# Cross-attention on one core: where chunk sums, shares, halves and weighted sums stand, and what they wait for

## The chip, the cores and the metric

The kernel runs on one core of a Trainium2 chip. The metric is device time in microseconds; the time before is the median of three runs. The core's engines are TensorE (PE in the views; its weight loads are PEld), VectorE (DVE), ScalarE (ACT), GpSimd (POOL) and SyncE (SP, here a queue of DMAs). Each works through its own list of instructions in order; semaphores order them among each other.

## The reference

```python
a = layer_norm(ctx, gamma, beta)                    # ctx: 32 x 375 x 512
Q = heads(x @ Wq.T); K = heads(a @ Wk.T); V = heads(a @ Wv.T)     # x: 32 x 112 x 512, 16 heads of 32
scores = einsum('bhtd,bhsd->bhts', Q, K) * 32 ** -0.5
attn = softmax(where(mask, scores, -inf))           # over the 375 context rows
out = heads_joined(einsum('bhts,bhsd->bhtd', attn, V)) @ Wo.T
return x + tanh(gate) * out
```

All is float32. The three projections of the main loop are made of three matmuls each, with high and low parts of both operands (`PASSES`).

## The kernel before

After a start (weights, queries of all sequences, kept in DRAM) comes a loop over 32 sequences of context, c, each with four slots of four heads. Two slots make a pair, m = 2c (even) or 2c + 1 (odd), 64 in all. Every engine has its own `slot_pair(m)`, written out by hand as one order, and they are skewed: what belongs to slots 2m and 2m + 1 on TensorE is exponentiated one pair later and weighted three pairs later.

**TensorE** (line 1291): K projection of slot 2m (12 matmuls into bank KB), V projection of one third of the context, or the output of an earlier sequence (12 into bank VO), K of slot 2m + 1, then a second V third (even m) or the output product `output(c - 3)` (odd m), the weighted sums of slots 2m - 6 and 2m - 5 (48 small matmuls into KB, line 1247) and the scores of 2m and 2m + 1 (line 1234). Outputs are tiles of 128 rows and sequences have 112, so `tile_of(b)` gives no tile for every eighth sequence: in the odd pairs 3, 5, 7 (nothing to put out yet), 23, 39 and 55 there is no output product. K of an even slot waits for the copy of the weighted sums out of KB (`pv_out`), the weighted sums wait for the copy of K out of KB (`k_done`). The last pair has the output of sequence 28 between its two K products.

**ScalarE** (line 804): exponentials of slot 2m - 3, second V copy or gated output, copy of the weighted sums (line 777, `weighted_out`; line 784 at the end), score copies with mask and scale (line 727), K copy (line 741), the high half of the normalised output of sequence c - 3 (line 754, even m), V copy (line 747), high part of the context (line 688), K copy, exponentials of slot 2m - 2 (line 736).

**VectorE** (line 1038): in odd pairs statistics of a later context (line 881) and the shares of sequence c - 2 (lines 986 to 992: adds up the parts, takes reciprocals, transposes), then joined maxima (line 947), row maxima of this pair's scores (line 961), spread (line 952) and subtraction (line 971) of the pair before, partial sums of the chunk sums (line 979).

**GpSimd** (line 594): sums of the three chunks of exponentials of slots 2m - 4 and 2m - 3 (lines 587 and 591, into one of two buffers `psum`), then in even pairs the product with the shares (line 567, `normalised`), the bias on the residual (line 553), the low half (line 575) and row statistics; in odd pairs the result (line 559). Then low parts of the context (line 547).

**SyncE** (line 452): the softmax maxima go through DRAM (`store_maxima`, `load_maxima`, lines 406 and 416), and so do the partial sums of a sequence (`store_parts`, `load_parts`, lines 423 and 430, even m) and the shares (`store_shares`, `load_shares`, lines 436 and 444, odd m). A wait on this queue holds all behind it.

The last three sequences (from `SUMMED` = 29 on) don't go through parts and shares: TensorE makes the denominators from the chunk sums (line 1254), VectorE reduces and spreads their reciprocals into `rspread` (`normalise`, lines 996 to 1002), and GpSimd multiplies (line 570). `o_norm` counts GpSimd's products, `o_done` its low halves.

## Time and profile before

| | us |
|---|---|
| median of 3 runs | 919.99 (919.9 to 923.03) |
| the profiled execution | 922.26 |
| its span, first to last instruction | 920.5 |
| matmuls on TensorE | 899.1 (98%) |
| VectorE / ScalarE / GpSimd | 760.7 / 678.3 / 630.1 |
| granted TensorE clock, mean | 0.996 |

The profile and its trace show one execution. Busy is what an engine executes; an idle time in brackets stands before the instruction that ended it, with the instruction that released it. Matmuls overlap, so their busy time isn't TensorE's peak, and the distance between equal groups is the better clock.

### The profile page before, as it was taken

The numbers are of one execution on the slowest core, as the hardware profiler recorded it, in microseconds if no ns is written. First come the engines' busy times: TensorE is split into PE (matmuls) and PEld (weight loads), VectorE is DVE, ScalarE is ACT, GpSimd is POOL, SyncE is SP. The second block draws the span as 40 slices with busy tenths as digits, with TensorE's granted clock in tenths as the row PEclk, the third lists the DMA queues.
The fourth block names the chain that finished last, engine by engine and source line by source line (L and its number), as shares of the span: only waits on it lengthen the run. The fifth ranks groups of instructions, "written<-read, shape, count | busy, mean of one in ns | idle before, by whom it ended". The sixth has DMA issues, their size and how long they took to land.

```text
span 920.5 us, 25302 instructions
## 1 busy us (share of the span) xinstructions
PE 899.1 (98%) x9747; PEld 780.0 (85%) x9747; DVE 760.7 (83%) x1498; ACT 678.3 (74%) x1304; POOL 630.1 (68%) x730
## 2 busy tenths in 40 slices
PE   8999999999999999999999999999999999999977
PEld 7899888888888888888888888888888888888865
DVE  6963398989888889888888888988888988988757
ACT  3422588878878778888878777877887877877854
POOL 0671466777777777687777677578787776677664
PEclk9999999999999999999999999999999999999989
DMA  9973143434455434445544444445555444544212
GB/s 283 367 245 151 48 98 99 110 95 110 117 128 132 114 104 104 121 117 132 133 114 104 122 125 108 111 102 125 131 133 132 113 102 127 125 101 105 66 31 68
DMA packets 109964, 114.03 MB, mean 124 GB/s; under 512 B 45716, under 2 KB 87604, under 8 KB 109844
## 3 DMA queue, kind: packets, MB, share of 16 engines
q1 hardware_dynamic: 109268, 111.49, 45.2%
q8 instruction: 77, 1.26, 0.6%
q10 hardware_dynamic: 576, 0.92, 0.3%
q14 instruction: 43, 0.35, 0.1%
HBM read 93.88 MB, written 18.50 MB: 122 GB/s over the span
## 4 chain that ended last, share of the span: by engine, by line
PE 73%; DMA 7%; DVE 6%; POOL 5%; ACT 5%; issue 2%; SPq 2%; POOLq 0%; DVEq 0%; ACTq 0%
PE banks L1089 50%; PE banks L1234 8%; PE banks L1112 8%; PE banks L1247 7%; DVE rmax L961 3%; DMA row_stats<-rmax 3%; ACT shared_q L736 3%; DMA part<-part_kept 2%; POOL shared_f L587 2%; ACT shared_q L727 1%; DMA shared_f<-in_xT 1%; POOL shared_f L591 1%; POOL xy L553 1%; POOL shared_r L575 1%; POOL shared_f L567 1%
## 5 line engine op out<-in xcount | busy, mean ns | idle before, releaser
L1089 PE MATMUL banks<-shared_r,w_k 128*128 128x376 f32 x1536 | 291.4, 338 | 2.7 <-ACT shared_f L777 2.7
L1089 PE MATMUL banks<-w_v,shared_r 128*125 128x512 f32 x1152 | 283.6, 395 | 0.0
L727 ACT ACTIVATE shared_q<-banks,maskT,rstd 125x448 f32<-125x448 f32 x384 | 243.4, 730 | 54.2 <-PE banks L1234 54.0
L1089 PEld LDWEIGHTS banks<-shared_r,w_k 128*128 128x128 f32 x1536 | 263.2, 188 | 16.2 <-issue 4.2
L961 DVE TRANSPOSE_TENSOR_REDUCE rmax<-shared_q 128x14 f32<-128x448 f32 x384 | 219.6, 618 | 60.3 <-ACT shared_q L727 59.2
L1089 PEld LDWEIGHTS banks<-w_v,shared_r 128*125 128x125 f32 x1152 | 212.4, 185 | 44.9
L971 DVE TENSOR_TENSOR shared_q<-shared_q,banks 125x448 f32<-125x448 f32 x384 | 207.8, 601 | 0.1
L587 POOL TENSOR_TENSOR shared_f<-shared_q 125x448 f32<-125x448 f32 x124 | 142.2, 1146 | 87.9 <-ACT shared_q L736 52.4
L736 ACT ACTIVATE shared_q<-shared_q 125x448 f32<-125x448 f32 x384 | 190.7, 570 | 10.7 <-DVE shared_q L971 10.4
L547 POOL TENSOR_TENSOR shared_r<-cn,shared_r 128x375 fp32r<-128x375 f32 x124 | 111.8, 923 | 90.4 <-ACT shared_r L688 90.3
L591 POOL TENSOR_TENSOR shared_f<-shared_f,shared_q 125x448 f32<-125x448 f32 x124 | 142.3, 1148 | 9.7
L1234 PE MATMUL banks<-shared_q,shared_f 32*125 32x112 f32 x3072 | 101.2, 275 | 0.0
L1234 PEld LDWEIGHTS banks<-shared_q,shared_f 32*125 32x125 f32 x3072 | 89.7, 183 | 11.6 <-issue 11.5
L1247 PEld LDWEIGHTS banks<-shared_q,shared_f 125*32 125x32 f32 x3072 | 71.2, 110 | 29.9 <-issue 20.9
L747 ACT ACTIVATE shared_f<-banks,rstd 125x512 f32<-125x512 f32 x96 | 65.5, 682 | 41.7 <-PE banks L1089 41.7
L1247 PE MATMUL banks<-shared_q,shared_f 125*32 125x112 f32 x3072 | 88.9, 261 | 5.4 <-ACT shared_f L741 4.0
L741 ACT ACTIVATE shared_f<-banks 128x376 f32<-128x376 f32 x128 | 63.6, 497 | 37.3 <-PE banks L1089 37.3
L1089 PE MATMUL banks<-w_o,shared_r 128*128 128x512 f32 x324 | 81.9, 403 | 5.7 <-POOL shared_r L575 5.7
L1112 PE MATMUL banks<-shared_r,wq 128*128 128x448 f32 x384 | 81.3, 371 | 1.3 <-DVE shared_r L856 1.3
L1112 PEld LDWEIGHTS banks<-shared_r,wq 128*128 128x128 f32 x384 | 71.9, 188 | 9.6 <-DVE shared_r L856 1.6
L1089 PEld LDWEIGHTS banks<-w_o,shared_r 128*128 128x128 f32 x324 | 61.4, 193 | 20.4 <-POOL shared_r L575 8.5
L952 DVE STREAM_TRANSPOSE banks<-top 128x448 f32<-128x448 f32 x128 | 73.1, 614 | 4.7 <-ACT shared_f L784 4.7
(101 smaller groups left out, 709.8 us busy)
## 6 DMA issues: line engine op xcount, KB each, us to landing
cn<-in_ctxT SPq DMA_DIRECT2D x128, 187.5 KB, 3.6
rows<-in_ctx SPq DMA_DIRECT2D x32, 720.0 KB
xy<-in_x SPq DMA_DIRECT2D x28, 256.0 KB, 7.1
q_kept<-shared_q SPq DMA_DIRECT2D x8, 896.0 KB, 6.7
shared_q<-q_kept SPq DMA_DIRECT2D x32, 224.0 KB, 4.1
out<-xy SPq DMA_DIRECT2D x28, 256.0 KB, 4.0
rshare<-share_kept SPq DMA_DIRECT2D x116, 56.0 KB, 2.4
shared_f<-in_xT SPq DMA_DIRECT2D x7, 896.0 KB, 11.1
```

Of the source, the lines that this page charges most:

```text
L547: pool.tensor_tensor(cT[:, p, 1, k, 0:S], cn[:, m % (2 * KT), :], cT[:, p, 0, k, 0:S].bitcast(F32), ALU.subtract) \
L587: pool.tensor_tensor(psum[0:SP_, h, :], prob[0:SP_, q, 0, :], prob[0:SP_, q, 1, :], ALU.add).then_inc(sum_half, 1)
L591: pool.tensor_tensor(psum[0:SP_, h, :], psum[0:SP_, h, :], prob[0:SP_, q, 2, :], ALU.add).then_inc(sum_done, 1)
L727: act.activation(prob[0:SP_, n % NB, j, :] .rearrange("p (a h t) -> p a h t", a=2, h=2), score_view(n, j), ACT.Identity, bias=maskT[0:SP_, ...
L736: act.activation(prob[0:SP_, n % NB, j, :], prob[0:SP_, n % NB, j, :], ACT.Exp, scale=SCALE).then_inc(exp_done, 1)
L952: dve.transpose(maxima_of(p).rearrange("p (k a) -> p k a", a=32), top[:, p % 2, :].unsqueeze(2).to_broadcast([128, BLK, 32])) \
L961: last = dve.tensor_reduce(rmax[:, n % 2, BLK * j:BLK * j + BLK], prob[:, n % NB, j, :].rearrange("p (k a) -> p k a", a=32), AX.X, ALU.max ...
L971: dve.tensor_tensor(prob[0:SP_, p % NB, j, :], prob[0:SP_, p % NB, j, :], maxima_of(p)[0:SP_, :], ALU.subtract).then_inc(sub_done, 1)
L1089: last = pe.matmul(dst, l, m, start=(start and k == 0), stop=(stop and k == len(pairs) - 1))
L1112: return pe.matmul(q_bank(g, m)[:, 0:GN], wq[:, a, k, 128 * m:128 * m + 128], xr[:, g, c, k, :], start=(k == 0 and e == 0), stop=(k == KT ...
L1234: last = pe.matmul(bank[banks[h]][0:SP_, T * places[h]:T * places[h] + T], kT[part, n % 2, SP_ * j:SP_ * j + SP_], qT[part, c % QB, u, :], ...
L1247: last = pe.matmul(dst[HD * h:HD * h + HD, :], v_sb[0:SP_, c % VB, j, col:col + HD], prob[0:SP_, p % NB, j, T * h:T * h + T], start=(j == ...
```

## The change

- `psum` gets four buffers instead of two. The chunk sums of slot p wait for the reader of slot p - 4 instead of p - 2.
- In the odd pairs without output product (3, 5, 7, 23, 39, 55) the weighted sums go to bank VO, which is idle there, and wait for the V copy instead of the K copy. K of the next pair no longer waits for their copy; V of the next pair does.
- `normalise` waits for `o_norm` only for the second of its two sequences; the buffer has no earlier reader for the first.
- SyncE: the shares are loaded right behind their store, the parts ahead of the loads of maxima.
- VectorE: shares ahead of statistics.
- GpSimd in even pairs: product, sum of slot 2m - 4, low half, sum of slot 2m - 3, bias. ScalarE: the high half ahead of the copy of the weighted sums.

```diff
--- before.py
+++ after.py
@@ -86,7 +86,7 @@
 
 
 
-        sizes = {"v": VB * ST * D, "pv": 8 * T, "den": 4 * T, "kT": 2 * SE, "sum": 2 * HT,
+        sizes = {"v": VB * ST * D, "pv": 8 * T, "den": 4 * T, "kT": 2 * SE, "sum": 4 * HT,
                  "free": 560}
         place, at = {}, 0
         for name, n in sizes.items():
@@ -108,7 +108,7 @@
         pv = cut_f("pv")
         den = cut_f("den")
         kT = cut_f("kT").rearrange("p (q s) -> p q s", q=2)
-        psum = cut_f("sum").rearrange("p (q n) -> p q n", q=2)
+        psum = cut_f("sum").rearrange("p (q n) -> p q n", q=4)
 
         rows = sb("rows", [128, ST, D])
         cn = sb("cn", [128, 2 * KT, S])
@@ -305,6 +305,11 @@
 
             return b - b // 8 if b > 0 else 0
 
+        def idle_bank(m):
+
+            c, odd = divmod(m, 2)
+            return odd and c < B - 1 and tile_of(c - 3) is None
+
         def pieces(b):
 
             at = b * T % RING
@@ -454,17 +459,15 @@
                 if summed(c - 2):
                     if odd:
                         store_shares(c - 2)
+                        load_shares(c - 2)
                     else:
                         store_parts(c - 2)
                 store_maxima(2 * m)
                 store_maxima(2 * m + 1)
+                if summed(c - 2) and not odd:
+                    load_parts(c - 2)
                 load_maxima(2 * m)
                 load_maxima(2 * m + 1)
-                if summed(c - 2):
-                    if odd:
-                        load_shares(c - 2)
-                    else:
-                        load_parts(c - 2)
                 for n in (2 * m + 8, 2 * m + 9):
                     if n < SLOTS:
                         load_ctx(sync, n)
@@ -578,12 +581,12 @@
 
             def sum_chunks(p):
 
-                q, h = p % NB, p % 2
+                q, h = p % NB, p % 4
                 pool.wait_ge(exp_done, p * ST + 2)
-                if p - 2 < SUMMED * KT:
-                    need(pool, part_done, p - 1)
+                if p - 4 < SUMMED * KT:
+                    need(pool, part_done, p - 3)
                 else:
-                    pool.wait_ge(pv_mm, p - 1)
+                    pool.wait_ge(pv_mm, p - 3)
                 pool.tensor_tensor(psum[0:SP_, h, :], prob[0:SP_, q, 0, :], prob[0:SP_, q, 1, :],
                                    ALU.add).then_inc(sum_half, 1)
                 pool.wait_ge(sum_half, p + 1)
@@ -595,15 +598,17 @@
                 c, odd = divmod(m, 2)
                 if m == 0:
                     mask_bias()
+                if not odd and c > 2:
+                    normalised(c - 3)
                 if pair(m - 2):
                     sum_chunks(2 * m - 4)
+                if not odd and c > 2:
+                    low_half(c - 3)
+                if pair(m - 2):
                     sum_chunks(2 * m - 3)
                 if not odd and m >= 0:
-                    if c > 2:
-                        normalised(c - 3)
-                        if tile_of(c - 3) is not None:
-                            add_bias(tile_of(c - 3))
-                        low_half(c - 3)
+                    if tile_of(c - 3) is not None:
+                        add_bias(tile_of(c - 3))
                     if m == PAIRS - 2:
                         normalised(B - 3)
                     if c + 1 < B and c > 0:
@@ -638,9 +643,9 @@
             for q in range(NB):
                 pool.memset(prob[96:128, q, :, :], LOWEST).then_inc(low_done, 1)
             pool.wait_ge(q_out, GROUPS * KT)
-            for q in range(2):
+            for q in range(4):
                 pool.memset(psum[96:128, q, :], 0.0).then_inc(low_done, 1)
-            pool.wait_ge(low_done, NB + 2)
+            pool.wait_ge(low_done, NB + 4)
             pool.wait_ge(c_done, KT)
             for m in range(-1, PAIRS):
                 slot_pair(m)
@@ -807,16 +812,16 @@
                     exponential(2 * m - 3)
                 if pair(m):
                     second_out(m)
+                if not odd and c > 2:
+                    high_half(c - 3)
                 if pair(m - 3):
-                    weighted_out(2 * m - 6)
+                    weighted_out(2 * m - 6, VO if idle_bank(m) else KB)
                 if pair(m):
                     scores_out(2 * m)
                 if pair(m):
                     scores_out(2 * m + 1)
                 if pair(m + 1):
                     k_out(2 * m + 2)
-                if not odd and c > 2:
-                    high_half(c - 3)
                 if pair(m + 1):
                     first_out(m + 1)
                 if m == PAIRS - 2:
@@ -977,7 +982,7 @@
                     need(dve, parts_stored, p // KT * 16)
                 u = p % KT
                 dve.tensor_reduce(parts[:, BLK * u:BLK * u + BLK],
-                                  psum[:, p % 2, :].rearrange("p (k a) -> p k a", a=32),
+                                  psum[:, p % 4, :].rearrange("p (k a) -> p k a", a=32),
                                   AX.X, ALU.add, apply_transpose=True).then_inc(part_done, 1)
 
             def shares(b):
@@ -998,7 +1003,8 @@
                 dve.wait_ge(dsum_done, b - SUMMED + 1)
                 dve.reciprocal(rden[:, :], dsum[:, :]).then_inc(rden_done, 1)
                 dve.wait_ge(rden_done, b - SUMMED + 1)
-                need(dve, o_norm, b)
+                if b > SUMMED:
+                    dve.wait_ge(o_norm, b)
                 dve.transpose(rspread[:, :].rearrange("p (k a) -> p k a", a=32),
                               rden[:, :].unsqueeze(2).to_broadcast([128, BLK, 32])) \
                     .then_inc(rspread_done, 1)
@@ -1037,14 +1043,14 @@
 
             def slot_pair(m):
                 c, odd = divmod(m, 2)
+                if odd and 0 <= c - 2 < SUMMED:
+                    shares(c - 2)
                 if odd and c + 2 < B and c + 2 > 2:
                     statistics(c + 2)
                 if m == 0:
                     statistics(2)
                 if m == PAIRS - 2:
                     normalise(B - 3)
-                if odd and 0 <= c - 2 < SUMMED:
-                    shares(c - 2)
                 if pair(m - 1):
                     join_maxima(2 * m - 2)
                     join_maxima(2 * m - 1)
@@ -1176,8 +1182,8 @@
                     if n == 0:
                         for w in "kvo":
                             pe.wait_ge(w_done[w], KT)
-                if n % 2:
-                    pe.wait_ge(k_done, n)
+                if n % 2 or idle_bank(n // 2 - 1):
+                    need(pe, k_done, n)
                 else:
                     need(pe, k_done, n)
                     need(pe, pv_out, n - 6)
@@ -1191,6 +1197,8 @@
 
                 if j == 0:
                     need(pe, y_out, tiles(c - 4))
+                    if c > 1 and idle_bank(2 * c - 1):
+                        pe.wait_ge(pv_out, 4 * c - 6)
                 need(pe, v_done, c * ST + j)
                 product(bank[VO][0:SP_, :],
                         [(cT[:, c % 2, d, k, SP_ * j:SP_ * j + SP_], wv[:, a, k, :])
@@ -1267,7 +1275,7 @@
                     return
                 for q in range(2):
                     pe.wait_ge(sum_done, p + q + 1)
-                    denominator(psum[:, q, :], to[:, (2 + q) * T:(3 + q) * T], True, True) \
+                    denominator(psum[:, (p + q) % 4, :], to[:, (2 + q) * T:(3 + q) * T], True, True) \
                         .then_inc(pv_mm, 1)
 
             def last_weighted_sums(p):
@@ -1305,8 +1313,11 @@
                 if odd and c < B - 1 and tile_of(c - 3) is not None:
                     output(c - 3, c * ST + ST)
                 if pair(m - 3):
-                    pe.wait_ge(k_done, 2 * m + 2)
-                    weighted_sums(2 * m - 6, bank[KB])
+                    if idle_bank(m):
+                        pe.wait_ge(v_done, c * ST + ST)
+                    else:
+                        pe.wait_ge(k_done, 2 * m + 2)
+                    weighted_sums(2 * m - 6, bank[VO if idle_bank(m) else KB])
                 if m == 0:
                     pe.wait_ge(mask_out, 1)
                 scores(2 * m)
```

On ScalarE, from the exponentials of an even pair on (736/741 exponentials, 747/752 V copy, 777/782 copy of the weighted sums, 727/732 score copies, 741/746 K copy, 754/759 high half; a change of line numbers alone shifts them by five). Before:

```order
L736 ACTIVATE shared_q<-shared_q 125x448 x6
L747 ACTIVATE shared_f<-banks,rstd 125x512
L777 ACTIVATE shared_f<-banks 128x224
L727 ACTIVATE shared_q<-banks,maskT,rstd 125x448 x6
L741 ACTIVATE shared_f<-banks 128x376
L754 ACTIVATE shared_r<-shared_f 128x4x112
L747 ACTIVATE shared_f<-banks,rstd 125x512
```

and now:

```order
L741 ACTIVATE shared_q<-shared_q 125x448 x6
L752 ACTIVATE shared_f<-banks,rstd 125x512
L759 ACTIVATE shared_r<-shared_f 128x4x112
L782 ACTIVATE shared_f<-banks 128x224
L732 ACTIVATE shared_q<-banks,maskT,rstd 125x448 x6
L746 ACTIVATE shared_f<-banks 128x376
L752 ACTIVATE shared_f<-banks,rstd 125x512
```

The high half moved from behind the K copy to ahead of the copy of the weighted sums.

On GpSimd, from the low parts of the context (547/550) at the end of an odd pair into an even one (587, 591/590, 594 chunk sums; 567/570 product; 553/556 bias; 575/578 low half, in two pieces here). Before:

```order
L547 TENSOR_TENSOR shared_r<-cn,shared_r 128x375 x2
L587 TENSOR_TENSOR shared_f<-shared_q 125x448
L591 TENSOR_TENSOR shared_f<-shared_f,shared_q 125x448
L587 TENSOR_TENSOR shared_f<-shared_q 125x448
L591 TENSOR_TENSOR shared_f<-shared_f,shared_q 125x448
L567 TENSOR_TENSOR shared_f<-shared_f,rshare 128x448
L553 TENSOR_TENSOR xy<-xy,gbo 128x512
L575 TENSOR_TENSOR shared_r<-shared_f,shared_r 128x4x96
L575 TENSOR_TENSOR shared_r<-shared_f,shared_r 128x4x16
```

and now:

```order
L550 TENSOR_TENSOR shared_r<-cn,shared_r 128x375 x2
L570 TENSOR_TENSOR shared_f<-shared_f,rshare 128x448
L590 TENSOR_TENSOR shared_f<-shared_q 125x448
L594 TENSOR_TENSOR shared_f<-shared_f,shared_q 125x448
L578 TENSOR_TENSOR shared_r<-shared_f,shared_r 128x4x96
L578 TENSOR_TENSOR shared_r<-shared_f,shared_r 128x4x16
L590 TENSOR_TENSOR shared_f<-shared_q 125x448
L594 TENSOR_TENSOR shared_f<-shared_f,shared_q 125x448
L556 TENSOR_TENSOR xy<-xy,gbo 128x512
```

Product and low half moved ahead of the first and of the second chunk sum.

On SyncE, from the store of the parts (423/428) in an even pair to the loads of the shares (444/449) in the odd one. Before:

```order
L423 DMA part_kept<-parts 4x32x56
L406 DMA row_stats<-rmax 4x32x42 x2
L416 DMA x_49<-row_stats 128x1x168
L416 DMA x_odd<-row_stats 128x1x168
L430 DMA part<-part_kept 32x224
L320 DMA cn<-in_ctxT 128x375 x2
L345 DMA out<-xy 128x512
L358 DMA shared_q<-q_kept 128x448
L436 DMA share_kept<-share_rows 32x2x32
L406 DMA row_stats<-rmax 4x32x42 x2
...
L444 DMA rshare<-share_kept 32x4x112 x4
```

and now:

```order
L428 DMA part_kept<-parts 4x32x56
L411 DMA row_stats<-rmax 4x32x42 x2
L435 DMA part<-part_kept 32x224
L421 DMA x_49<-row_stats 128x1x168
L421 DMA x_odd<-row_stats 128x1x168
L325 DMA cn<-in_ctxT 128x375 x2
L350 DMA out<-xy 128x512
L363 DMA shared_q<-q_kept 128x448
L441 DMA share_kept<-share_rows 32x2x32
L449 DMA rshare<-share_kept 32x4x112 x4
L411 DMA row_stats<-rmax 4x32x42 x2
```

The parts' load moved ahead of both loads of maxima, the shares' loads from behind them to ahead of the stores of the odd pair's maxima.

## Rows read from the trace of the kernel before

**Rows 1.** The page: busy us, share of the span, instructions.

```profile
PE 899.1 (98%) x9747; PEld 780.0 (85%) x9747; DVE 760.7 (83%) x1498; ACT 678.3 (74%) x1304; POOL 630.1 (68%) x730
```

**Rows 2.** TensorE's timeline, score groups: start, length, instruction, [idle before].

```profile
697.91 1.58 PE L1234 MATMUL banks<-shared_q,shared_f 32*125 32x112 f32 x48
...
710.54 1.58 PE L1234 MATMUL banks<-shared_q,shared_f 32*125 32x112 f32 x48
...
723.24 1.58 PE L1234 MATMUL banks<-shared_q,shared_f 32*125 32x112 f32 x48
```

**Rows 3.** TensorE's timeline, pairs 39 to 41: sums, scores, K, K.

```profile
580.41 1.36 PE L1247 MATMUL banks<-shared_q,shared_f 125*32 125x112 f32 x48 [0.57 <-ACT shared_f L741]
581.70 1.58 PE L1234 MATMUL banks<-shared_q,shared_f 32*125 32x112 f32 x48
583.54 2.31 PE L1089 MATMUL banks<-shared_r,w_k 128*128 128x376 f32 x12 [0.27 <-ACT shared_f L777]
...
594.72 1.84 PE L1234 MATMUL banks<-shared_q,shared_f 32*125 32x112 f32 x48
596.95 2.30 PE L1089 MATMUL banks<-shared_r,w_k 128*128 128x376 f32 x12 [0.39 <-ACT shared_f L777]
```

**Rows 4.** TensorE's timeline, score groups around odd pair 35.

```profile
519.61 1.58 PE L1234 MATMUL banks<-shared_q,shared_f 32*125 32x112 f32 x48
...
533.13 1.58 PE L1234 MATMUL banks<-shared_q,shared_f 32*125 32x112 f32 x48
```

**Rows 5.** TensorE's timeline, last pair.

```profile
875.13 1.58 PE L1234 MATMUL banks<-shared_q,shared_f 32*125 32x112 f32 x48
...
883.31 5.49 PE L1089 MATMUL banks<-w_o,shared_r 128*128 128x512 f32 x12 [4.35 <-POOL shared_r L575]
...
893.36 1.58 PE L1234 MATMUL banks<-shared_q,shared_f 32*125 32x112 f32 x48
```

**Rows 6.** Timelines of GpSimd, VectorE and ScalarE in the last two pairs.

```profile
875.19 1.13 POOL L587 TENSOR_TENSOR shared_f<-shared_q 125x448 f32<-125x448 f32 x1 [7.12 <-PE banks L1254]
...
881.04 0.65 DVE L1002 STREAM_TRANSPOSE rspread<-rden 128x448 f32<-128x448 f32 x1 [4.22 <-POOL shared_f L567]
...
895.00 3.80 ACT L727 ACTIVATE shared_q<-banks,maskT,rstd 125x448 f32<-125x448 f32 x6
```

**Rows 7.** Timelines of VectorE and ScalarE, pair 39, and VectorE, pairs 49, 50.

```profile
585.91 0.56 DVE L986 TENSOR_REDUCE whole_sum<-part 32x56 f32<-32x224 f32 x1 [1.21 <-DMA part<-part_kept]
...
596.46 0.35 ACT L777 ACTIVATE shared_f<-banks 128x224 f32<-128x224 f32 x1
...
709.26 1.84 DVE L881 BATCH_NORM_STATS2 stats<-rows 125x6 f32<-125x512 f32 x3
...
725.72 0.65 DVE L961 TRANSPOSE_TENSOR_REDUCE rmax<-shared_q 128x14 f32<-128x448 f32 x1 [1.93 <-ACT shared_q L727]
```

**Rows 8.** Timelines of GpSimd and ScalarE, even pairs without a gap.

```profile
697.49 1.14 POOL L587 TENSOR_TENSOR shared_f<-shared_q 125x448 f32<-125x448 f32 x1 [2.63 <-ACT shared_q L736]
...
703.59 0.61 ACT L754 ACTIVATE shared_r<-shared_f 128x448 fp32r<-128x448 f32 x1
...
723.43 0.36 ACT L777 ACTIVATE shared_f<-banks 128x224 f32<-128x224 f32 x1 [0.30 <-issue]
```

**Rows 9.** Tiles `part`, then `share_kept`: idle us, times; landing of DMAs.

```profile
  DMA part<-part_kept: 29.1, 21
...
DMA to landing us min/median/max: 2.9/3.8/4.2
...
DMA to landing us min/median/max: 1.4/2.4/3.6
```

**Rows 10.** SyncE's queue, pairs 48 and 49: start, length of the issues.

```profile
702.27 2.35 SPq L406 DMA_DIRECT2D row_stats<-rmax  x2
...
708.19 0.43 SPq L430 DMA_DIRECT2D part<-part_kept  x1
...
720.46 1.86 SPq L444 DMA_DIRECT2D rshare<-share_kept  x4
```

## What I predict, and why

> **What bounds the kernel now.** I read the page first: TensorE's matmuls are busy 899.1 us of a 920.5 us span, VectorE 760.7, ScalarE 678.3 [rows 1]. The reader is to see that only TensorE can be the bound, and that only its idle time, about 21 us, can be had. Then TensorE as a clock. Each of the 64 slot pairs ends with one group of score matmuls (line 1234), so the distance between two such groups is the cost of a pair: 710.54 - 697.91 = 12.63 us for an odd pair with an output projection, 723.24 - 710.54 = 12.70 for an even one [rows 2]. These are pairs without a gap. Every longer pair lost something, and I went through all of them.
>
> Three kinds of loss come out. (a) In the odd pairs whose output product is missing (m = 3, 5, 7, 23, 39, 55) there is a gap of 0.57 in front of the weighted sums, and 0.27 in front of the K product behind the scores [rows 3]: 0.84 in each of six, 5.0 us. (b) Odd pairs that wait for the low half of the output's operand: 533.13 - 519.61 = 13.52 instead of 12.63 [rows 4], 0.9 lost. Read so, nine pairs (9, 25, 27, 35, 40, 41, 43, 47, 57) lose 0.73, 0.33, 0.52, 0.90, 0.27, 0.93, 0.22, 0.47, 0.94: 5.3 us. (c) The last pair takes 893.36 - 875.13 = 18.23 us, with 4.35 of waiting for GpSimd's low half in it [rows 5]. The other 25 us behind it are one chain of latencies that the change doesn't touch.
>
> **Part by part: the end.** In pair 62 VectorE may spread its reciprocals only at 881.04, after 4.22 us idle, because the spread waits for `o_norm`, which here guards nothing [rows 6]. GpSimd stands 7.12 us before its chunk sums, since with two buffers they wait for the denominators of two slots earlier; then sums, product, bias and low half follow one another, TensorE's output product waits for them, ScalarE's copies for that, and its score copies of the last pair start at 895.00 [rows 6]. Now (my working, with these durations): with four buffers GpSimd is free at 866.9. The product with the shares goes first, and the sum of slot 120 ends at 874.5. ScalarE's high half is over at 875.2, the low half 1.13 later, at 876.4. TensorE's first K ends at 878.8 and finds the operand ready. Output to 881.7, second K to 883.7, 0.6 for its copy, weighted sums and denominators to 886.0. VectorE spreads at 877.0, reduces the maxima from 878.3 to 881.6, spreads and subtracts to 885.9, which is what the third score group needs. So the scores of the last pair start at 886.0, not 893.36: 7.4. ScalarE's exponentials then end at 887.2 and its score copies start at 887.75 against 895.00 [rows 6]: 7.25. I take 7.2. From below: if the spread's wait alone went, 4.2; nothing in these rows gives a loss.
>
> **The idle bank.** The weighted sums now wait for the V copy, asked for a whole K product (2.1 us) behind V, and the copy of their own bank is wanted only at V of the next pair. That gives TensorE the 0.84. But who is next? VectorE. From the subtraction before the idle pair on it has no idle time but the 1.21 us for the parts [rows 7]; behind that wait shares, maxima, subtraction, then ScalarE's exponentials, V copy and the copy of the weighted sums at 596.46 run in a row, and K in pair 41 had to wait 0.39 us for that copy and started at 596.95 [rows 3, 7]. The new order takes the wait for the parts away (below), so the copy could come 1.2 us earlier, but the high half (0.61, [rows 8]) now stands in front of it: 596.46 - 1.2 + 0.6 = 595.86, and K, 0.49 behind as before, at 596.35. Without any wait it could start at 596.95 - 0.57 - 0.27 - 0.39 - 0.27 (by which the scores before it were stretched) = 595.45. So K starts 0.6 us earlier than before and not 1.5: 0.9 is given back as a wait for ScalarE's copy. The same working gives -0.1 for pair 23, where the parts were waited for 0.19, and 0 for pair 55 (0.57). The waits of class (b) that stood in pairs 25, 41 and 57 go: 0.3, 0.5, 0.6. In the first stretch (pairs 3 to 9) the first idle pair has no high half behind it and keeps its 0.84, the other two I give 0.2 each, the mean of the three worked out, and pair 9 the same 0.3 as pair 25: 1.5, an estimate. Together 1.5 + 0.2 + 1.1 + 0.6 = 3.4 us. Ends: 0 (all given back) and 5.0 + 3.2 (no give-back, and the whole of class (b) in pairs 9, 25, 40, 41 and 57).
>
> **The parts and shares.** VectorE waits 29.1 us in 21 places for the parts' load, whose landing takes 2.9 to 4.2 us [rows 9]. SyncE issues it behind both loads of maxima (708.19; the stores were out at 704.62, and then their landing is waited for) [rows 10]. Moved ahead of them it goes out at 704.7 and lands at 708.5 (median 3.8), when VectorE has just ended the chunk sums and turns to what follows at 709.26 [rows 7, 10]; that the statistics (some 2.2 us) no longer cover it costs nothing then. Queued behind it are the loads of maxima, 0.43 us, inside a wait. In odd pairs the shares are done 3 us earlier, at 710.6, but SyncE now stands for the landing of their store before the four loads and the stores of maxima. 0.33 issue + 2.4 landing + 1.9 for four issues [rows 9, 10] end at 715.2; the first maxima of that pair are ready at 715.1. So it is free by a hair; at the worst landing of 3.6 the stores of maxima are 1.3 us late, and VectorE, which waited 1.93 us for ScalarE ahead of the next maxima [rows 7], takes that up. Bounds: 0 to 1.3 us in those three pairs that follow an idle one and have no such slack, at most 4.
>
> The Trainium skill bears on this. *DMA: Bandwidth & Descriptors*, section on latency and other measured facts, says that HBM latency is 0.2 us on average and 2 us at high load and dominates a DMA's fixed cost. This store now goes out right behind two context loads, an output store and a Q load, so by the page it could land some 2 us later than the quiet 2.4, at 4.4. The trace's own spread (1.4 to 3.6) is what I go by; by the page the three pairs would pay the 4 us above and the sum would be 8.7 instead of 12.7.
>
> **Low half and high half.** GpSimd's product, low half and one chunk sum swap places: before, the low half was behind both chunk sums, the product and the bias. Now the product runs in GpSimd's idle time before the first chunk sum (2.63 us) and the low half follows that sum, some five us earlier. ScalarE's high half moves into the 0.30 us of idle time ahead of the copy of the weighted sums [rows 8]; that copy ends at 724.1 instead of 723.8, and K wants it behind the scores, 723.24 + 1.51 = 724.75 [rows 2, 8]. So class (b) goes in the remaining pairs 27, 35, 43, 47: 0.52 + 0.90 + 0.22 + 0.47 = 2.1. If the cover went (high half late by more than 0.65) each us costs a us of TensorE in 28 even pairs. The four chunk buffers free GpSimd of 25.3 us of waiting for VectorE and the two extra memsets lie in front of the first pair, where GpSimd has no reader: 0.
>
> **Sum.** 7.2 + 3.4 + 2.1 = 12.7 us. The profiled execution, 922.26 us with a span of 920.5, becomes 909.6 with 907.8. The median of the three runs, 919.99, stands 2.3 under that execution; the same 12.7 off it: 907.3.
>
> **Rivals.** (1) All gaps close: 5.0 + 5.3 + 7.2 = 17.5, 902.5. For it: TensorE's gaps are all traced to things the change moves. Against: rows 7, VectorE has no slack behind an idle pair. 0.17. (2) Only the end comes, since VectorE, or SyncE waiting for its shares, takes the place of the waits in mid-kernel: 919.99 - 7.2 = 912.8. 0.21. (3) The change doesn't do what it says at the end: GpSimd, not the spread, still sets the low half, and gains are 4 us or less: 916 and more, no change. Against it rows 5 and 6, which show both waits separately. 0.08. (4) Slower: ScalarE's high half now stands ahead of the copies that TensorE's K product needs, and waits for GpSimd's product, and that for the shares' loads. I have them land at 717.6, wanted by 722.6 (723.1, less 1.16 for the product, plus 0.65 of margin). Should SyncE be held so long that they land as before, 720.46 + 1.86 + 2.4 = 724.7, K would wait 2.1 us in 28 even pairs, 59 us; half of that, 30 us, with the 12.7 off, gives 937. It decides from a landing 5 us later than worked out, beyond every landing in rows 9. 0.04. The forecast has 0.50.
>
> The range reaches just past rivals 1 and 2: 902 to 913. A measurement can tell some 0.5%, 4.6 us, from no change: faster 0.50 + 0.17 + 0.21 = 0.88, no change 0.08, slower 0.04.
>
> **What would show it.** The last pair between score groups 11 us long instead of 18.2; idle pairs at 10.0 instead of 10.5, K two pairs later waiting about 0.9 us for ScalarE's copy; the wait for parts under 8 us instead of 29.1; no wait for GpSimd's low half; SyncE's stores of maxima in odd pairs within 1 us of the maxima. Wrong would be a new wait of K in ordinary even pairs, or VectorE's wait for x and x_odd (22.5 us now) doubled.

## The result and the profile after

| | before | after |
|---|---|---|
| median, us | 921.51 (4 runs, 919.9 to 924.25) | 907.35 (4 runs, 906.91 to 908.5) |
| ratio of the runs, 95% interval | 1 | 0.9845, 0.9815 to 0.9876 |
| the profiled execution / its span | 922.26 / 920.5 | 906.91 / 905.1 |
| first to last score group (64 pairs) | 793.5 | 779.2 |

The kernel is 14.2 us faster by the medians, and 15.4 by the two profiled spans: 14.3 of them lie between the first and the last score group, 1.1 in the start and the tail. I use that distance, the loop, for all that follows, since the start varies with the input DMAs: it does so by 3 us in one run below.

The page after: busy us and share of the span by engine, and the chain that ended last, which now runs on TensorE for 85% of the span (73% before, where DMAs had 7%):

```profile
PE 894.3 (99%) x9747; PEld 779.1 (86%) x9747; DVE 763.1 (84%) x1498; ACT 672.1 (74%) x1304; POOL 633.3 (70%) x732
...
PE 85%; DVE 9%; ACT 4%; issue 1%; DMA 0%; POOL 0%; ACTq 0%; DVEq 0%; POOLq 0%; SPq 0%
```

TensorE's timeline after, pairs 39 to 41, the answer to [rows 3]: start, length, instruction, [idle before]. The gaps of 0.57 and 0.27 are gone, the K product of pair 41 waits 0.61 instead of 0.39.

```profile
575.10 1.36 PE L1255 MATMUL banks<-shared_q,shared_f 125*32 125x112 f32 x48
576.39 1.66 PE L1242 MATMUL banks<-shared_q,shared_f 32*125 32x112 f32 x48
577.97 2.33 PE L1095 MATMUL banks<-shared_r,w_k 128*128 128x376 f32 x12
...
591.39 2.30 PE L1095 MATMUL banks<-shared_r,w_k 128*128 128x376 f32 x12 [0.61 <-ACT shared_f L782]
```

The pair of [rows 4] after, 528.46 - 515.84 = 12.62 us, and the last pair of [rows 5], 878.46 - 867.58 = 10.88, with an output product of 2.90 us where it took 5.49:

```profile
515.84 1.58 PE L1242 MATMUL banks<-shared_q,shared_f 32*125 32x112 f32 x48
...
528.46 1.58 PE L1242 MATMUL banks<-shared_q,shared_f 32*125 32x112 f32 x48
...
867.58 1.58 PE L1242 MATMUL banks<-shared_q,shared_f 32*125 32x112 f32 x48
869.09 2.33 PE L1095 MATMUL banks<-shared_r,w_k 128*128 128x376 f32 x12
871.25 2.90 PE L1095 MATMUL banks<-w_o,shared_r 128*128 128x512 f32 x12
...
878.46 1.58 PE L1242 MATMUL banks<-shared_q,shared_f 32*125 32x112 f32 x48
```

SyncE's queue in pairs 48 and 49 after, the answer to [rows 10]: the parts' load is out 0.1 us behind the stores, and VectorE waits for it nowhere.

```profile
695.52 2.35 SPq L411 DMA_DIRECT2D row_stats<-rmax  x2
697.97 0.42 SPq L435 DMA_DIRECT2D part<-part_kept  x1
...
703.90 0.33 SPq L441 DMA_DIRECT2D share_kept<-share_rows  x1
706.64 1.86 SPq L449 DMA_DIRECT2D rshare<-share_kept  x4
708.61 1.92 SPq L411 DMA_DIRECT2D row_stats<-rmax  x2
```

The landing of the tile `part` after, from its issue, answering to [rows 9] (2.9/3.8/4.2 before):

```profile
DMA to landing us min/median/max: 1.9/2.0/2.3
```

The second landing in [rows 9] counts 116 loads of shares and 29 stores together. The store alone (line 436 before, line 441 after), before and then after:

```profile
DMA to landing us min/median/max: 1.4/1.5/2.4
...
DMA to landing us min/median/max: 1.6/2.5/4.0
```

By pairs (a pair ends with its scores), where the 14.3 us went:

| pairs | before | after | difference | predicted |
|---|---|---|---|---|
| 3 to 9 | 84.02 | 81.75 | 2.3 | 1.5 |
| 23 to 25 | 36.51 | 36.08 | 0.4 | 0.2 |
| 39 to 41 | 37.38 | 35.99 | 1.4 | 1.1 |
| 55 to 57 | 37.13 | 36.33 | 0.8 | 0.6 |
| 27, 35, 43, 47 | 52.58 | 50.49 | 2.1 | 2.1 |
| 63 | 18.23 | 10.88 | 7.35 | 7.2 |
| the other 42 timed pairs | | | 0.0 | 0 |

### The profile page after: what moved, and what is told of

Read it like the earlier page. It is cut to its first block, busy times and chain, and to the rows that moved or that the text cites. A ratio compares the mean times of both kernels' runs of the same rounds, so it can differ in the third digit from the quotient of the medians.

```text
span 905.1 us, 25298 instructions
## 1 busy us (share of the span) xinstructions
PE 894.3 (99%) x9747; PEld 779.1 (86%) x9747; DVE 763.1 (84%) x1498; ACT 672.1 (74%) x1304; POOL 633.3 (70%) x732
## 4 chain that ended last, share of the span: by engine, by line
PE 85%; DVE 9%; ACT 4%; issue 1%; DMA 0%; POOL 0%; ACTq 0%; DVEq 0%; POOLq 0%; SPq 0%
PE banks L1095 59%; PE banks L1242 9%; PE banks L1118 9%; PE banks L1255 7%; DVE rmax L966 3%; ACT shared_q L741 2%; DVE shared_q L976 2%; DVE banks L957 1%; ACT shared_q L732 1%; DVE stats L886 1%; DVE parts L984 0%; PE banks L1162 0%; ACT shared_f L752 0%; DMA x_odd<-row_stats 0%; DVE top L952 0%
## 5 line engine op out<-in xcount | busy, mean ns | idle before, releaser
L966 DVE TRANSPOSE_TENSOR_REDUCE rmax<-shared_q 128x14 f32<-128x448 f32 x384 | 222.8, 627 | 74.4 <-ACT shared_q L732 72.9
L741 ACT ACTIVATE shared_q<-shared_q 125x448 f32<-125x448 f32 x384 | 188.5, 568 | 7.6 <-DVE shared_q L976 7.6
L1095 PE MATMUL banks<-w_o,shared_r 128*128 128x512 f32 x324 | 78.2, 390 | 0.0
```

The lines of the kernel that those rows point to most:

```text
L741: act.activation(prob[0:SP_, n % NB, j, :], prob[0:SP_, n % NB, j, :], ACT.Exp, scale=SCALE).then_inc(exp_done, 1)
L966: last = dve.tensor_reduce(rmax[:, n % 2, BLK * j:BLK * j + BLK], prob[:, n % NB, j, :].rearrange("p (k a) -> p k a", a=32), AX.X, ALU.max ...
L1095: last = pe.matmul(dst, l, m, start=(start and k == 0), stop=(stop and k == len(pairs) - 1))
```

## The experiments

All ratios are to the kernel before, run on the same chip. In the table "loop" is the distance from the first to the last score group in the profiled execution. It is one execution of each kernel. How far it can wander shows in the kernel before, e9 and e10, which have the same order everywhere ahead of the last pairs: without the last pair their loops are 775.3, 778.9 and 777.9. Differences of a few us against a kernel with that order are to be read together with the ratios.

| run | median, us | ratio, 95% interval | loop |
|---|---|---|---|
| changed kernel | 907.35 | 0.9845 (0.9815 to 0.9876) | 779.2 |
| e1 without the idle bank | 908.96 | 0.9848 (0.9824 to 0.9872) | 781.0 |
| e2 old order of product and halves | 911.42 | 0.9873 (0.9847 to 0.9899) | 783.8 |
| e3 shares' loads late | 963.49 | 1.0425 (1.0385 to 1.0466) | 834.8 |
| e4 two buffers | 907.65 | 0.9838 (0.9809 to 0.9867) | 779.4 |
| e5 parts' load late | 925.18 | 1.0044 (1.0018 to 1.0071) | 794.1 |
| e6 spread waits | 907.33 | 0.9849 (0.9815 to 0.9883) | 779.2 |
| e7 high half behind the copy | 905.72 | 0.9837 (0.9805 to 0.9869) | 777.2 |
| e8 the same, statistics late in idle pairs | 904.35 | 0.9817 (0.9783 to 0.9851) | 776.1 |
| e9 before, new order in pair 62 only | 917.67 | 0.9947 (0.9928 to 0.9967) | 791.5 |
| e10 before, spread free only | 923.46 | 1.0007 (0.9987 to 1.0026) | 795.5 |
| e11 before, parts and shares early only | 917.11 | 0.9949 (0.9934 to 0.9964) | 788.4 |
| e12 before, e9 and e11 together | 909.39 | 0.9863 (0.9836 to 0.989) | 781.3 |

**e1, the idle bank away.**

```diff
-            return odd and c < B - 1 and tile_of(c - 3) is None
+            return False
```

> The changed kernel, with the weighted sums of the idle pairs back in bank KB and with the waits that go with it. Theory 1 (TensorE's two gaps of 0.57 and 0.27 in six places are what the bank removes, and a part is given back two pairs later): the pairs 3, 5, 23, 39, 55 take 10.54 us again and each pair behind them 13.02, while the waits of K in pairs 25, 41, 57 (0.70, 0.61, 0.75 in the changed kernel) shrink to under 0.3; the span is 905.1 + 3 = 908, between 907 and 909.5. Rival (the bank gives nothing, all mid-kernel gain is from the new order on GpSimd, ScalarE and SyncE): span within 0.5 us of 905.1, with the gaps of 0.57 moved elsewhere. Second rival (all 5.0 us are the bank's, nothing is given back): 910.

Pairs 3, 5, 39 take 10.54 to 10.57 again and the even ones behind them 13.00 to 13.02, and pairs 25 and 41 take 12.62: no wait of K in them. The loop is 1.8 us longer, so theory 1 holds: the bank takes away 5.0 us of gaps and 3.2 of them are lost again, 2.9 of these as five waits of K for ScalarE's copy.

**e2, the old order of product and halves** on GpSimd and ScalarE, in all pairs.

> The changed kernel with the old order on GpSimd (both chunk sums, product, bias, low half) and on ScalarE (high half behind the K copy); buffers, bank, SyncE's order and the free spread stay new. Theory 1 (the low half's place is what removes TensorE's waits for it in mid-kernel and most of the wait in the last pair): waits of the output product for the low half come back, 1 to 3 us in mid-kernel, and some 3.5 us in the last pair (low half ends near 882.3 less 7.5 on this clock, product wants it 3.5 us before); K's waits in pairs 25, 41, 57 shrink to about 0.1, 2 us gained; span 905.1 + 3.5 + 2 - 2 = 908.6, between 907 and 911. Rival (four buffers and earlier shares alone make the low half early enough, the order is without effect): span 903 to 905.5 and no wait of the last output product.

The total is as expected and its parts aren't. In mid-kernel no wait for the low half comes back: pairs 27, 35, 43, 47 stay at 12.62. The last pair takes 17.69 us. TensorE's waits in e2 have a single one for the low half, the last pair's:

```profile
PE banks L1093 <- POOL shared_r L578: 3.7, 1, 3.7
```

So the new order is worth 6.8 us in the last pair. In mid-kernel it costs 2.2 us, since pairs 9, 25, 41 take 12.62 or 12.63 without it. My explanation of the 2.1 us in pairs 27 to 47 fell here; e5 and e11 look for the right one.

**e3, the shares' loads late.** In SyncE's loop `load_shares(c - 2)` stands behind both `load_maxima` again.

> The changed kernel with the four loads of the shares back behind both loads of maxima. Theory 1 (the early loads are the cover under which product and high half could be moved ahead): the loads land some 5 us later, GpSimd's product starts near 724.7 on the old clock instead of 720, ScalarE's high half holds the copy of the weighted sums, and K waits 1 to 2.5 us in each of some 27 odd pairs: span 905 + 30 to 60, 935 to 965. Rival (SyncE's order is without effect, GpSimd's product has room enough): span 904 to 907.

The loop is 55.6 us longer. TensorE's waits in e3 have one large line, for the copy (total us, count, longest):

```profile
PE banks L1096 <- ACT shared_f L783: 45.2, 28, 4.2
```

The timelines of GpSimd, ScalarE and TensorE in one even pair of e3: product late for the shares, high half late for the product, copy behind it, K behind that.

```profile
464.76 1.14 POOL L571 TENSOR_TENSOR shared_f<-shared_f,rshare 128x448 f32<-128x448 f32 x1 [3.29 <-DMA rshare<-share_kept]
...
465.93 0.67 ACT L760 ACTIVATE shared_r<-shared_f 128x192 fp32r<-128x192 f32 x2 [1.52 <-POOL shared_f L571]
466.50 0.34 ACT L783 ACTIVATE shared_f<-banks 128x224 f32<-128x224 f32 x1
...
466.98 2.32 PE L1096 MATMUL banks<-shared_r,w_k 128*128 128x376 f32 x12 [0.88 <-ACT shared_f L783]
```

**e4, two buffers**, and **e6, the spread waits:** one edit undone in each. This is e6's:

```diff
-                if b > SUMMED:
-                    dve.wait_ge(o_norm, b)
+                need(dve, o_norm, b)
```

> The changed kernel with two buffers of chunk sums again. Theory 1 (four buffers are worth little by themselves: GpSimd's waits for VectorE's partial sums were cover, and in the end the product with the shares goes ahead of the sums anyway): mid-kernel pairs unchanged within 0.5 us in all; in the end GpSimd waits for the denominators again until they are done, sum 121 and with it the product of sequence 29 come 3 us later, ScalarE's high half ahead of the second K copy holds that by some 2 us: span 907, between 905.5 and 908.5. Rival (the four buffers carry the end): the last pair takes 14 us or more again, span 908.5 to 912.

> The changed kernel with the old wait for o_norm in front of the first spread. Theory 1 (the product with the shares now goes first in the pair, so that the wait is over before VectorE comes to it, and freeing the spread is without effect beside the new order): span 905.1 within 0.4 us, last pair 10.9 us. Rival (the freed spread carries the 4.2 us that VectorE stood there before): last pair 13 us or more, span 907.5 to 909.5.

Neither does anything: loops of 779.4 and 779.2, last pairs of 11.03 and 10.88. In e4 the ScalarE delay of 2 us that I expected at the end is 0.15.

**e5, the parts' load late**, behind both loads of maxima, with VectorE's shares still first.

> The changed kernel with the parts' load back behind both loads of maxima (shares still ahead of the statistics on VectorE). Theory 1 (the early load of the parts is what took VectorE's lateness and with it the waits of mid-kernel away; the order of GpSimd and ScalarE did not, as the run with the old order showed): VectorE waits some 3 us for the parts in each of 29 odd pairs, since 2.2 us of statistics no longer cover it, its subtractions and ScalarE's exponentials are late by as much, and with 0.65 us of margin K waits 0.5 to 1.5 us in some 25 pairs: span 917 to 940. Rival (SyncE's order of the parts is without effect, the shares' order alone matters): span 905 to 907.

The loop is 14.9 us longer; the span of 920.4 lies near the foot of the expected range. From e5's tile `part`: VectorE waits in all 29 odd pairs, and the landing takes 3.7 us again. TensorE then waits 7.5 us in 12 places for the copy, where I expected some 25, and 5.5 in 5 for subtractions. It waits nowhere for the low half, which keeps its new place here: the late load comes out at other operands.

```profile
  DMA part<-part_kept: 53.0, 29
...
DMA to landing us min/median/max: 2.7/3.7/4.1
```

**e9, e10, e11, e12** start from the kernel before and add one thing or two. From e9's edit, the lines added on GpSimd:

```diff
+                if m == PAIRS - 2:
+                    normalised(c - 3)
+                    sum_chunks(2 * m - 4)
+                    low_half(c - 3)
+                    sum_chunks(2 * m - 3)
```

> The kernel before, with the new order on GpSimd (product, sum, low half, sum) and ScalarE (high half ahead of the copy) in pair 62 alone; two buffers, the waiting spread and all else old. Theory 1 (in the end it is the order that counts, neither buffers nor the freed spread): the last pair takes 10.9 to 11.2 us instead of 18.2, the span is shorter by 7, ratio to the kernel before 0.992. Rival (with two buffers GpSimd still stands until the denominators of pair 62 are done, and the spread waits): last pair 14 us or more, 4 us or less come off.

> The kernel before with the freed spread alone. Theory 1 (TensorE's output product waits for the low half on GpSimd, which this doesn't move): last pair 17.6 to 18.2 us, 0 to 0.6 us come off. Rival (the prediction's lower bound for the end): 4.2 us come off, last pair 14 us.

> The kernel before with SyncE's new order (parts ahead of the loads of maxima, shares right behind their store) and VectorE's shares ahead of the statistics; two buffers, bank KB, old orders on GpSimd and ScalarE. Theory 1 (the waits for the low half in mid-kernel came from VectorE's lateness by the parts' load, not from the order on GpSimd): pairs 27, 35, 43, 47 take 12.6 us, pairs 25, 41, 57 under 13, VectorE waits under 3 us for parts; 4 to 5.3 us come off, the last pair keeps 17.7 to 18.3. Rival (it takes the low half's new place or the four buffers to be rid of them): under 2.5 us come off.

> The kernel before with two edits only: SyncE's parts and shares early with VectorE's shares first, and the new order on GpSimd and ScalarE in pair 62 alone; bank KB, two buffers, waiting spread. Theory 1 (these two carry the gain outside the idle bank): pairs 27, 35, 43, 47 at 12.6 us, last pair 11 us since VectorE is on time there too, 781 to 782 us from the first to the last score group, as in the changed kernel without its bank; span 906.5 to 908. Rival (the last pair needs the four buffers or the freed spread as well and stays at 12.6, as in the run with the order at the end only): 783 us, span 908.5 to 910.

e10: the last pair takes 17.62 instead of 18.23, and the whole is the same as before. e11: all odd pairs with an output from 9 to 53 at 12.62 to 12.65, pair 57 at 12.88, last pair 18.14; TensorE's only wait for the low half is the 4.36 of the last pair. e9: the last pair takes 12.59, neither theory's number. GpSimd stood waiting, not for denominators but for the shares, whose loads are late in this kernel (e9's timeline of GpSimd):

```profile
879.32 1.13 POOL L567 TENSOR_TENSOR shared_f<-shared_f,rshare 128x448 f32<-128x448 f32 x1 [7.59 <-DMA rshare<-share_kept]
```

With both edits, e12, the last pair takes 11.06 and the loop 781.3, 0.3 from e1, which has all of the change but the bank. So of the 14.3 us, 5.1 are SyncE's and VectorE's order (e11), 7.1 the new order of GpSimd and ScalarE in pair 62 on top of it (e12), 1.8 the bank (e1), and 0.3 buffers, spread and the new order in mid-kernel. By the medians e11 gains 4.8 us (3.3 to 6.1 by its interval) and e12 12.9 (10.1 to 15.1), which agrees. The bank's share depends on the order around it: without the last pair, e2 (bank, old order) takes 766.1 and e12 (no bank, old order ahead of pair 62) 770.3. With the old order in mid-kernel the bank is worth about 4, and the new order takes 2.2 of that back. A kernel with e12's edits and the bank alone was not run.

**e7 and e8, a better place for the high half.** e7 in ScalarE's loop; e8 also has the statistics of the six idle pairs behind the partial sums on VectorE.

```diff
+                if pair(m - 3):
+                    weighted_out(2 * m - 6, VO if idle_bank(m) else KB)
                 if not odd and c > 2:
                     high_half(c - 3)
-                if pair(m - 3):
-                    weighted_out(2 * m - 6, VO if idle_bank(m) else KB)
```

> The changed kernel with ScalarE's high half behind the copy of the weighted sums, ahead of the score copies, where ScalarE stands 1.1 us waiting for TensorE. Theory 1 (the waits of K in pairs 7, 9, 25, 41, 57, 0.25 to 0.75 us each, are this high half in front of a copy that is late behind an idle pair): they shrink to under 0.15 each, 2.3 to 2.9 us come off, everything else stays: span 902.2 to 902.8, ratio to the kernel before about 0.981. Rival (the waits are VectorE's lateness, and the high half is only beside them): span within 0.7 of 905.1. A second rival: the high half now holds the score copies and with them VectorE's maxima, and what K gains comes back at the scores: 905.

> As the kernel with the high half behind the copy, and in the six idle pairs VectorE's statistics also behind the partial sums instead of ahead of the maxima. Theory 1 (once the high half is out of the way TensorE has no waits left behind idle pairs but 0.3 us in pair 55 and some hundredths elsewhere): 0 to 0.8 us better than without this edit, span 901.8 to 902.8. Rival (VectorE, without slack behind an idle pair, still holds TensorE): 1.5 us or more come off.

e7: pairs 25, 41, 57 at 12.82 to 12.86 (13.28 to 13.42 with the changed kernel), the loop 2.0 us shorter, where I expected 2.3 to 2.9; waits of up to 0.2 stay. Its profiled execution has a longer span, 906.4, since its first score group came 3.2 us later: TensorE waited 2.23 us for its first inputs. e8: every odd pair with an output but 61 at 12.62, the loop 3.1 us shorter than the changed kernel's, median 904.35 with runs from 903.91 to 904.71. The statistics gave 1.1 where I expected at most 0.8. ScalarE in pair 40 of the changed kernel: the copy (L782) stands behind the high half (L759).

```profile
589.86 0.67 ACT L752 ACTIVATE shared_f<-banks,rstd 125x512 f32<-125x512 f32 x1
590.43 0.56 ACT L759 ACTIVATE shared_r<-shared_f 128x448 fp32r<-128x448 f32 x1
590.90 0.34 ACT L782 ACTIVATE shared_f<-banks 128x224 f32<-128x224 f32 x1
```

ScalarE there in e8: the copy comes first, and the high half is done before ScalarE stands waiting for TensorE anyway.

```profile
587.20 0.68 ACT L752 ACTIVATE shared_f<-banks,rstd 125x512 f32<-125x512 f32 x1
588.19 0.36 ACT L782 ACTIVATE shared_f<-banks 128x224 f32<-128x224 f32 x1 [0.31 <-issue]
588.44 0.57 ACT L759 ACTIVATE shared_r<-shared_f 128x448 fp32r<-128x448 f32 x1
589.65 3.81 ACT L732 ACTIVATE shared_q<-banks,maskT,rstd 125x448 f32<-125x448 f32 x6 [0.64 <-PE banks L1244]
```

e8 is the fastest of all: its four runs end at 904.71, and those of e6, which does nothing and ran on the same chip, begin at 906.73.

## Why the prediction came out as it did

The time, 907.3, was met at 907.35, partly by luck: the sum was 12.7 off a median of 919.99 that turned out 921.51 with one more run, and the gain is 14.2. The mechanism was right for the end and for the bank. It was wrong for the rest of mid-kernel.

**The end** was right in size (7.2, measured 7.35) and in its chain: GpSimd's sum began at 864.72, the low half at 867.62, and TensorE found its operand, as worked out. What fell is the lower bound, 4.2 us for the freed spread: e10 gives 0.6 in that pair. VectorE's 4.22 us of waiting were real, but what it releases was not what TensorE waited for; TensorE waited for the low half. I took an idle time next to the path for one on it. Nor did the buffers matter (e4), which I had made the first step of the chain: with the product ahead of the sums, a sum that starts when the denominators are done is early enough (e12, 11.06).

**The idle bank** has the right mechanism, gaps closed and most of it given back at ScalarE's copy, and the give-back was oversized: 0.9 a time, measured waits of 0.61 to 0.74, and in all 3.4 us predicted for these pairs, 4.9 measured. In pairs 3 to 9 (1.5, an estimate; 2.3) the working gave back 0.64 twice, and the two waits are 0.62 and 0.25; of the 0.7 that pair 9 had lost it counted only 0.3. Pair 5 kept all it gained, and pair 7 gained nothing (10.54, now 10.58). In pairs 39 to 41 two sizes were off. The high half puts the copy back by 0.47 us (590.43 to 590.90 in the rows of pair 40), not by 0.61. And VectorE's subtraction starts 1.36 us earlier, not 1.2 (counted from the scores of pair 38: 592.13 - 571.16 before, 586.10 - 566.49 after). What holds the copy in the end is two things: moving the high half alone gives 2.0 of the 3.2 us back (e7), moving VectorE's statistics another 1.1 (e8). With both, the loop is 4.9 us shorter than without the bank (e1), of the 5.0 that the gaps were.

**The remaining class (b) waits,** 2.1 us, measured 2.1, had the wrong cause, so this number is luck. The prediction put them down to the place of the low half. e2 has the old place and none of the waits, e11 has nothing of the new place and none either, and e5 brings mid-kernel losses back: they came from VectorE standing for the parts' load. The step "GpSimd's product, low half and one chunk sum swap places, so class (b) goes" is the one that failed.

The first error was in reading class (b) as waits for the low half. In the kernel before TensorE waits for it 5.7 us in 7 places, 4.35 of them in the last pair, so some 1.4 of the 5.3 us in mid-kernel. In pairs 9, 35, 41 and 57 K also waited for ScalarE's copy, 1.1 us in all. Pair 35 shows the chain, on VectorE, GpSimd and twice TensorE:

```profile
510.49 0.56 DVE L986 TENSOR_REDUCE whole_sum<-part 32x56 f32<-32x224 f32 x1 [2.67 <-DMA part<-part_kept]
...
520.63 1.13 POOL L587 TENSOR_TENSOR shared_f<-shared_q 125x448 f32<-125x448 f32 x1 [4.07 <-ACT shared_q L736]
...
521.52 2.30 PE L1089 MATMUL banks<-shared_r,w_k 128*128 128x376 f32 x12 [0.33 <-ACT shared_f L777]
...
528.86 3.06 PE L1089 MATMUL banks<-w_o,shared_r 128*128 128x512 f32 x12 [0.19 <-POOL shared_r L575]
```

A late VectorE made late exponentials; these made a late copy for K, late sums, and so a late low half. VectorE's waits for the parts ahead of pairs 27, 35, 43 and 47 were 2.07, 2.67, 2.41 and 2.11 us; of the other 17 only one, 2.09 ahead of pair 59, was as long. In e9 and e10 other ordinary pairs lose (29, 31, 33, 49 and 51 among them), each right behind a wait for the parts of 1.7 us or more.

**Parts and shares.** The predicted wait for the parts was under 8 us, it is 0; landings were 2.0 us, not the 3.8 I carried over, because the load no longer leaves behind the loads of maxima (e5, with it behind them again, has 3.7). The 2.4 us for the landing of the shares' store was misread: it is the median of stores and loads together. The store alone took 1.5 before and takes 2.5 now, so the term was met by luck. VectorE's wait for x and x_odd rose from 22.5 to 30.0 us and didn't double.

The Trainium skill (*DMA: Bandwidth & Descriptors*, latency and other measured facts) puts HBM latency at 0.2 us on average and 2 us at high load. By the prediction's estimate from it the store would land at 4.4. The store, which now leaves closer behind the Q load (0.6 us in pair 40, 2.9 before), did land later, by 1.0 us in the median and 1.6 at the longest (4.0 for 2.4), and so by less than 2 us. That the load is the cause isn't shown, since no run varied it.

**Rival 4,** slower if the shares come late, was priced at 59 us, 28 waits of K of 2.1 each, for loads where they stood before; e3 is that case and has 55.6. The 28 waits are there, but 24 of them take 0.8 to 1.9 us and the other four 3.0 to 4.2, in the pairs behind the idle ones; together 45.2. So the price is near by its total, not pair by pair. The cover is real: the new order on GpSimd and ScalarE in all even pairs can't stand without SyncE's.

## What to carry to other kernels

Of an engine near its limit, measure the distance between equal groups of work, list what every longer one lost, and then ask of each late operand which engine was late first: here it was three engines back. An edit that frees a wait beside the path gives next to nothing (e10, e6), and an edit that moves work ahead of a copy which the bound engine needs belongs behind that copy if there is idle time behind it (e7). Undo each part of a change alone and then add the few that matter to the old kernel: the new loads with VectorE's order, and the new order of GpSimd and ScalarE in one pair, held 12.2 of 14.3 us (e12).

## What was not expected of the hardware

A wait of TensorE cost more than itself. Stretches of 4 us of the kernel before, with busy us of PE, PEld, DVE, ACT, POOL, then the granted clock:

```profile
878.00:882.00 4.00, 0.96 (x6) 0.65 (x4) 0.96 (x3) 3.52 (x7) 3.92 (x4) 1.00 0.00 0
882.00:886.00 4.00, 2.69 (x6) 2.15 (x7) 4.00 (x10) 0.00 (x0) 2.35 (x3) 0.55 0.03 5
886.00:890.00 4.00, 4.00 (x14) 3.38 (x13) 4.00 (x9) 1.17 (x3) 0.00 (x0) 0.60 0.32 81
```

The same view of e10, behind a wait of 2.09 us inside the scores of pair 40:

```profile
600.00:603.00 3.00, 3.00 (x12) 3.00 (x12) 2.80 (x6) 3.00 (x6) 2.87 (x3) 0.56 0.73 203
```

TensorE's clock has two levels, 1.2 and 2.4 GHz, shown as 0.50 and 1.00; a stretch in between has some of both. Behind the 4.35 us of waiting in the last pair it was granted at 0.55 and 0.60, so mostly the lower, and the output product took 5.49 us where it takes 2.90 at full clock: of the 7.35 us won in the last pair 4.35 are the wait, 2.6 this product, the rest mostly the K product behind it (2.52 for 2.22). In e10 the K product behind a wait of 2.09 us took 3.58 instead of 2.32. Behind gaps of 0.2 to 0.75 us no such stretch shows. e3 has many waits of K to compare: behind the four of 2.98 to 4.16 us its product took 3.75 to 4.10 us, and behind 23 of the 24 of 0.83 to 1.93 it took 2.29 to 2.32. The one exception, behind a wait of 1.72 in pair 53, took 3.85. Stretches of e3 with the K product behind a wait of 1.93 and behind that one:

```profile
440.00:443.00 3.00, 2.29 (x13) 2.32 (x14) 1.72 (x3) 3.00 (x7) 2.92 (x3) 1.00 0.95 209
...
788.00:792.00 4.00, 3.74 (x13) 3.77 (x14) 3.13 (x6) 3.81 (x7) 3.84 (x5) 0.57 0.82 179
```

So the length of the wait alone doesn't decide it here; what does stays open.

The kernel before ran from 917.3 to 926.7 us over all its runs, the changed one from 906.9 to 908.5. Kernels with the parts' load late wander most: e5, e9 and e10 by 8.3, 7.7 and 5.6 us in ten runs each, e11 and e12 by 1.6 and 1.5 in four.
